# Three passes over the edges of a graph: all row gathers on POOL, and the preparation inside the first pass

## The chip, the cores and the metric

The kernel runs on one core of one Trainium2 chip. The metric is the device time of one execution in microseconds, and the kernel's time is the median of its runs. A profile comes from one execution of its own; its span is the time from the first recorded instruction to the last.

## The reference

Two graph networks follow one another on a graph of N = 12,500 nodes with C = 96 features and 412,500 directed edges (src, dst), sorted by dst. `edge_attr_4` has 4 numbers an edge, `edge_weight1` one.

```python
# first network (its edge input is the one weight an edge), two convolutions with e shared
e = relu(edge_attr @ W_l0 + b_l0) @ W_l1 + b_l1
def gine_conv(x, W1, b1, W2, b2):
    agg = segment_sum(relu(x[src] + e), dst)
    return relu(relu((x + agg) @ W1 + b1) @ W2 + b2)
x = layernorm(x + h2)                 # h2: relu of the second convolution of relu of the first
# second network; mlp(h) = gamma * (h - mean) * rsqrt(var + eps) + beta of relu(h @ W + b), over all rows
message = mlp(concat([x[src], x[dst], mlp(edge_attr_4)]))
x = layernorm(x + segment_sum(message, dst) + mlp(x))
```

So each of three passes over all edges reads one row of 96 numbers by src for every edge, adds a term of the edge, applies a function and sums by dst. The means and variances over all edges are taken in the passes too.

## The kernel before

**Tiling.** The edges stand in tiles of P = 128 (one a partition), T = 26 tiles make a slab, and there are S = 124 slabs. A slab is worked through in 7 chunks, six of CH = 4 tiles and one of 2. V = 4 slabs, that is Q = 28 chunks, are one iteration of a loop written out in full; 31 iterations are one pass. `edge_pass` builds three of them: the first (names conv0_..., table x_rows), the second (conv1_..., table h_rows; `stats=True`, it also takes the statistics of the edge features, from the loads of ea_parts) and the last (last_..., table p_rows). Each has a form for windows, which the data allow and which runs, and a general one that does not run here. `finish` closes the kernel.

**Who does what in a pass.** POOL gathers the rows of a tile with one indirect DMA: `gather`, L268, called from `gpsimd_windows` (L1278 ff.), 26 tiles a slab into one of four buffers `got[j]`, by the node numbers in `idx[j]`. Before the tiles of a chunk it waits until VectorE has added the same chunk of the iteration before (semaphore `add`), and before a slab also for its node numbers (`idx`, L265 loads them). TensorE computes per chunk the hidden layer of the edge term (L540), the product into `ps_pre` (L1314) and the sums by destination; VectorE adds the gathered rows to `ps_pre` (`add_gathered`, L638, once a chunk, signals `add`), cuts the result into parts (L586, L597) and makes the one-hot matrices (L1390); ScalarE applies the relus. Per-chunk matters run one behind another over the engines with semaphores, without an order fixed beyond each engine's own program.

**SyncE's program** (`sync_windows`, L1151 ff.) sets the order around the change. For each slab it runs `next_idx` (loads the node numbers of the slab two further on, after waiting in `landed` for the gathers that read the old ones), then `slab_rows` (after waiting until the hidden layer of the slab two back is done: three loads of w_parts or ea_parts, six in the second pass, L520 and L526), then, from the second slab of the iteration on, `far_rows`. The last tile of the iteration's fourth slab (FAR_J = 3, FAR_T = 25) isn't gathered by POOL: `far_idx_load` brings its 128 node numbers, and `far_rows` reads them into registers, 8 at a time (L1209), and issues one DMA of one row for each (L1213), 42, 43 and 43 at three places. The first place waits until all adds of the iteration before are done. Thus POOL gathers 103 of an iteration's 104 tiles. VectorE waits for the rows (semaphore `far`) before the last add of the fourth slab.

**The preparation** is a block of its own, "setup" (L294 ff.): node numbers and first rows of the nodes are loaded, POOL gathers the first two slabs (52 tiles), VectorE computes window bases, counts what falls outside the windows (`inside`, float32) and the verdict `fits`, writes `near`, and clears the last rows of `sums` (L408). Two small products on TensorE have banks of their own. After the block's end all engines begin the first pass, whose programs start with clearing buffers (L651 to L654) and cutting the weights into bf16 parts (L678).

**The row of counts.** `sums` has a row C for counts. After the second pass's loop POOL clears it (`zero_counts`, L1111, called in `gpsimd_end`) for the last pass.

Of the kernel before, what the change touches and what calls it, by code (L numbers as in the profile page):

```python
# [18 lines left out]
F32 = mybir.dt.float32  # L19
# [6 lines left out]
P = 128  # L26
# [10 lines left out]
FAR_J, FAR_T = V - 1, T - 1  # L37
FAR_PLACES = V - 1
FAR_LOAD = 8
# [113 lines left out]
def gnn_kernel(nc, a, out):  # L153
# [22 lines left out]
    with ctx:  # L176
# [117 lines left out]
        with ExitStack() as st:  # L294
            dst_i = sb("dst_i", [P, S * T], I32, st)
            dst_n = sb("dst_n", [S, T * P], I32, st)
            near_f = sb("near_f", [S, T * P], F32, st)
            near_b = sb("near_b", [S, T * P], BF16, st)
            inside = sb("inside", [P, T * P], F32, st)
            heads = sb("heads", [1, HEADS], I32, st)  # L300
            heads_s = sb("heads_s", [S, NC_], I32, st)
            head_s = sb("head_s", [S, NC_], F32, st)
            head_f = sb("head_f", [1, HEADS], F32, st)
            base_f = sb("base_f", [1, S], F32, st)
            due = sb("due", [1, S], F32, st)
            ahead = sb("ahead", [1, S], F32, st)
            ps = pools(st, base=1, count=1)
            s = Sems(st, "setup")
# [10 lines left out]
            @block.sync  # L319
            def _(sp):  # L320
                for j in range(V):
                    load_slab_idx(sp, early_idx[j], j, early[f"idx{j}"])
                sp.dma_start(heads[:], a["heads"]).then_inc(s["heads"], 16)
                sp.dma_start(heads_s[:], a["heads_s"]).then_inc(s["heads"], 16)
                sp.dma_start(due[:], a["due"]).then_inc(s["heads"], 16)
                sp.dma_start(dst_i[:], a["dst_t"]).then_inc(s["dst"], 16)
                sp.dma_start(dst_n[:], a["dst_n"]).then_inc(s["near"], 16)
                sp.wait_ge(s["near"], 32)
                sp.dma_start(near, near_b[:]).then_inc(early["nearout"], 16)
                sp.wait_ge(early["nearout"], 16)  # L330

            @block.scalar
            def _(act):

                act.dma_start(w_parts[3:4, :], a["is_edge"]).then_inc(s["ones"], 16)
                act.dma_start(ea_parts[3 * D:3 * D + 1, :], a["is_edge"]).then_inc(s["ones"], 16)
                act.wait_ge(s["dst"], 16)
                act.wait_ge(s["near"], 32)
                act.dma_start(sums[0:C, :], a["x_cols"]).then_inc(early["cols"], 16)
                act.wait_ge(s["ones"], 32)  # L340

            @block.tensor
            def _(pe):
                pe.wait_ge(s["base"], 1)
                pe.matmul(ps["base"][0][:, 0:S], ones[0:1, :], base_f[:], start=True, stop=True).then_inc(s["pe"], 1)
                pe.wait_ge(s["cnt"], 1)
                pe.matmul(ps["count"][0][:, 0:4], ones[:], tmp[:, 10:14], start=True, stop=True).then_inc(s["pe"], 1)

            @block.vector
            def _(v):  # L350
                go, done = chain(v, s["dve"])
# [4 lines left out]
                v.wait_ge(s["heads"], 48)  # L356
# [6 lines left out]
                v.drain().then_inc(s["base"], 1)  # L363
                go(v.tensor_copy(base_i[:], base_f[:]))
                go(v.tensor_copy(head_i[:], head_f[:]))
                v.wait_ge(s["dst"], 16)
# [6 lines left out]
                v.wait_ge(s["pe"], 1)  # L373
                go(v.tensor_copy(base_all[:], ps["base"][0][:, 0:S]))
                done()
                rel3 = rel[:].rearrange("p (s t) -> p s t", t=T)
                go(v.tensor_tensor(rel3, rel3, ps["base"][0][:, 0:S].unsqueeze(2).to_broadcast([P, S, T]), ALU.subtract))
# [9 lines left out]
                v.wait_ge(s["near"], 16)  # L387
# [5 lines left out]
                v.tensor_copy(near_b[:], near_f[:]).then_inc(s["near"], 16)  # L393
                count(12, near_f[:], 0.0)
                count(13, near_f[:], float(R))
                v.drain().then_inc(s["cnt"], 1)
                v.wait_ge(s["pe"], 2)
                go(v.tensor_copy(tmp[0:1, 4:8], ps["count"][0][0:1, 0:4]))
# [10 lines left out]
                done()  # L409


        def edge_pass(name, table, y=None, split_edges=False, stats=False, last=False):
# [8 lines left out]
            with ExitStack() as st:  # L421
                idx = early_idx
# [10 lines left out]
                far_idx = sb(f"{name}_far_idx", [1, P], I32, st)  # L433
# [44 lines left out]
                if split_edges:  # L478
                    cols = sb("cols", [C, STEP], F32, st)
                    rows_out = sb("h1_out", [P, NODE_TILES * C], F32, st)  # L480
                    w_f = sb(f"{name}_w_f", [P, COLS], F32, st)
                    w_p = [sb(f"{name}_w_p{i}", [P, COLS], BF16, st) for i in range(3)]
                    e_f = sb(f"{name}_e_f", [P, D * PIECE], F32, st)
                    e_p = sb(f"{name}_e_p", [P, 3 * D * PIECE], BF16, st)
                    hid_f = [sb(f"hid_f{i}", [k, C], F32, st) for i, k in enumerate((KW, KE))]
# [1434 lines left out]
```

## Time and profile before

| | us |
|---|---|
| median of 3 runs | 20690.47 (20690.3 to 20700.37) |
| the profiled execution | 20513.53 |
| its span | 20511.7 |
| TensorE's mean granted clock in it | 0.66 |

The profile gives, for each engine (PE is TensorE, PEld its weight loads, DVE VectorE, ACT ScalarE, POOL GpSimd, SP SyncE), busy time and instructions; a q behind a name (SPq) means the instructions that the engine's sequencer handles, such as the issue of a DMA. Line numbers are those of the kernel before. In a row of the timeline stand the start, the duration, the engine, the line, the operation with output and input, and in brackets how long the engine was idle before it and what ended that. "issue" there is idleness for which the profile shows no cause, "remote" one that ended with another engine's signal. A row of the stretches (windows) counts the instructions of one line that start in a stretch.

### The profile page before, as it was taken

The page shows a single profiled execution, that of the slowest core. Times are in us where ns is not written, and L with a number is a line of the kernel's source. Part 1 is how long each engine was busy: PE and PEld are TensorE (multiplying, and loading weights), DVE is VectorE, ACT ScalarE, POOL GpSimd, SP SyncE. Part 2 cuts the span into 40 slices and gives each one's busy share as a digit, 9 for nine tenths or more (in the row PEclk, how much of TensorE's full clock was granted, in tenths as well). Part 3 has the DMA queues.
Part 4 walks back from the last instruction along what each step waited for, and adds up shares of the span by engine and source line. Part 5 has one row for each costly group of instructions (what it writes and reads, how often), then busy time and mean ns, then how long its engine had stood idle before and what let it go on. Part 6 is the DMA issues. An engine that isn't in the chain of part 4 may idle for free. (4 is left out here: it accounts for less than half of the span.)

```text
span 20511.7 us, 195475 instructions
## 1 busy us (share of the span) xinstructions
PE 9556.3 (47%) x34164; PEld 6799.3 (33%) x34164; DVE 7552.5 (37%) x15603; ACT 4963.2 (24%) x11020; POOL 9073.7 (44%) x9633
## 2 busy tenths in 40 slices
PE   3444444444454554555555555634344434443444
PEld 2333333333333333333333333422233323322333
DVE  3232223232232333333333333434344444443445
ACT  1121212122121222222222222222222222222223
POOL 4444444444444444444444444344444444444443
PEclk9999999999998555555555555555555555555555
DMA  2111111111111111111111111111111111111111
GB/s 61 30 28 31 29 31 29 31 29 31 30 29 40 31 31 30 32 33 33 32 33 32 33 33 32 29 34 29 31 30 30 30 30 30 29 29 31 29 29 33
DMA packets 615379, 650.24 MB, mean 32 GB/s; under 512 B 446921, under 2 KB 447402, under 8 KB 613947
## 3 DMA queue, kind: packets, MB, share of 16 engines
q0 software_dynamic: 306528, 471.44, 10.9%
q1 hardware_dynamic: 256342, 144.36, 2.9%
q10 hardware_dynamic: 51712, 27.54, 0.5%
q14 instruction: 750, 6.14, 0.1%
q8 instruction: 47, 0.77, 0.0%
HBM read 604.73 MB, written 39.43 MB: 31 GB/s over the span
## 5 line engine op out<-in xcount | busy, mean ns | idle before, releaser
L1314 PE MATMUL ps_pre<-w_e,conv_hid 97*128 97x96 f32 x12896 | 3281.4, 434 | 3688.8 <-issue 2145.0
L1314 PEld LDWEIGHTS ps_pre<-w_e,conv_hid 97*128 97x128 f32 x12896 | 2878.0, 327 | 4421.1 <-issue 4029.8
L1314 PE MATMUL ps_pre<-last_w_q,last_hid 128*128 128x96 f32 x6448 | 1628.1, 432 | 2747.0 <-issue 1720.4
L268 POOL DMA_INDIRECT early_got<-p_rows,early_idx x1612 | 1520.7, 943 | 2441.8 <-issue 1449.0
L268 POOL DMA_INDIRECT early_got<-h_rows,early_idx x1612 | 1521.4, 944 | 2190.8 <-issue 1414.2
L1314 PEld LDWEIGHTS ps_pre<-last_w_q,last_hid 128*128 128x128 f32 x6448 | 1440.3, 327 | 3132.6 <-issue 2479.4
L638 DVE TENSOR_TENSOR ps_pre<-ps_pre,early_got 128x384 f32<-128x384 f32 x1302 | 698.0, 536 | 4808.9 <-remote 2284.1
L268 POOL DMA_INDIRECT early_got<-in_x_rows,early_idx x1612 | 1525.0, 946 | 1952.6 <-issue 1243.7
L579 ACT ACTIVATE conv_part<-ps_pre 128x384 bf16<-128x384 f32 x1736 | 815.9, 470 | 5996.6 <-DVE ps_pre L638 3514.7
L268 POOL DMA_INDIRECT conv_got<-h_rows,early_idx x1581 | 1491.5, 943 | 1604.5 <-issue 1383.6
L268 POOL DMA_INDIRECT last_got<-p_rows,early_idx x1581 | 1492.0, 944 | 1530.7 <-issue 1530.4
L268 POOL DMA_INDIRECT conv_got<-in_x_rows,early_idx x1581 | 1491.6, 943 | 1446.8 <-issue 1445.6
L540 PE MATMUL ps_hid<-conv_row,w_hid 12*96 12x512 bf16 x1736 | 1086.2, 626 | 1794.2 <-issue 1346.3
L603 PE MATMUL ps_win<-conv_part,conv_hot 128*112 128x288 bf16 x6448 | 1907.0, 446 | 0.6 <-DVE conv_part L597 0.5
L553 ACT ACTIVATE conv_hid<-ps_hid 96x512 f32<-96x512 f32 x1736 | 974.2, 561 | 3554.5 <-DMA dst_n<-in_dst_n 1126.2
L1390 DVE TENSOR_TENSOR conv_hot<-ps_own,rel 128x448 bf16<-128x448 f32 x1736 | 1018.0, 586 | 1534.1 <-remote 1083.0
L638 DVE TENSOR_TENSOR ps_pre<-ps_pre,conv_got 128x384 f32<-128x384 f32 x868 | 465.6, 536 | 2408.4 <-remote 1597.0
L603 PEld LDWEIGHTS ps_win<-conv_part,conv_hot 128*112 128x112 bf16 x6448 | 1291.2, 214 | 78.2 <-DVE conv_part L597 2.5
L540 PE MATMUL ps_hid<-last_row,w_hid 40*128 40x512 bf16 x868 | 493.7, 569 | 1361.9 <-DVE last_hid L1362 681.4
L540 PEld LDWEIGHTS ps_hid<-conv_row,w_hid 12*96 12x96 bf16 x1736 | 260.1, 150 | 2513.3 <-issue 2095.8
L625 DVE BATCH_NORM_STATS2 conv_parts<-conv_feat 96x6 f32<-96x512 f32 x868 | 564.4, 650 | 1164.6 <-issue 593.8
L603 PE MATMUL ps_win<-last_part,last_hot 128*112 128x291 bf16 x3224 | 964.0, 450 | 0.6 <-DVE last_part L597 0.5
(255 smaller groups left out, 11507.6 us busy)
## 6 DMA issues: line engine op xcount, KB each, us to landing
conv_got<-in_x_rows SPq DMA_DIRECT2D x3968, 0.4 KB
conv_got<-h_rows SPq DMA_DIRECT2D x3968, 0.4 KB
last_got<-p_rows SPq DMA_DIRECT2D x3968, 0.4 KB
conv_row<-ea_parts SPq DMA_DIRECT2D x372, 84.5 KB
last_row<-ea_parts SPq DMA_DIRECT2D x372, 84.5 KB
early_got<-in_x_rows,early_idx POOLq DMA_INDIRECT x1612
early_got<-h_rows,early_idx POOLq DMA_INDIRECT x1612
early_got<-p_rows,early_idx POOLq DMA_INDIRECT x1612
```

The lines of the kernel that those rows point to most:

```text
L268: gp.indirect_dma_start(to[:, t * C:(t + 1) * C], None, table, bass.IndirectOffsetOnAxis(index[:, t:t + 1], 0)).then_inc(sem, 16)
L540: pe.matmul(ps["hid"][0][0:HC, 0:nt * P], w_hid[:], row[r][AT:AT + K, t0 * P:(t0 + nt) * P], start=True, stop=True).then_inc(s["hid"], 1)
L553: act.activation(hid[b][0:C, 0:nt * P], ps["hid"][0][0:C, 0:nt * P], ACT.Relu).then_inc(s["rhid"], 1)
L579: act.activation(part_of(q, 0, nt)[:, :, 0:C], m3, ACT.Relu).then_inc(s["part0"], 1)
L603: return pe.matmul(bank[0:W, 0:3 * M].rearrange("p (i c) -> p i c", i=3), hot_b[:, t * W:(t + 1) * W], parts, start=start, stop=stop)
L625: v.bn_stats(parts[:, c * 6:(c + 1) * 6], feat[b][:, 0:nt * P]).then_inc(s["bn"], 1)
L638: v.tensor_tensor(at, at, got[j][:, t0 * C:(t0 + nt) * C], ALU.add).then_inc(s["add"], 1)
L1314: mm = pe.matmul(ps["pre"][q % 2][:, t * C:(t + 1) * C], hid[q % 2][0:P if last else C1, t * P:(t + 1) * P], w_q[j % U][:, c * C:(c + 1) * ...
L1390: v.tensor_tensor(hot[q % 2][:, 0:nt * W].rearrange("p (t w) -> p t w", w=W), iota[:, 0:W].unsqueeze(1).to_broadcast([P, nt, W]), rel[:, b ...
```

## The change

Three things are changed.

1. POOL gathers all 104 tiles of an iteration. `far_idx_load`, `far_rows`, their buffer and their waits go, on SyncE and on VectorE.
2. The preparation is no block of its own any more. A class `Preparation` holds its buffers, and its parts stand at the head of the first pass's programs. Its buffer `inside` is bf16, its two products go to the bank `ps["e"]`. SyncE loads the preparation's data, then the weights, stores `near`, loads the constants, and waits for `nearout` and for VectorE's new signal `set_fits` before it branches into the windows' form; POOL gathers the first 52 tiles and then waits for `set_fits` too. ScalarE copies the weights before it loads x_cols.
3. VectorE clears the row of counts at the head of the second pass (in `prepare`), where POOL did at its end.

```diff
-FAR_J, FAR_T = V - 1, T - 1
-FAR_PLACES = V - 1
-FAR_LOAD = 8
-def group_tiles(g, j=None):
+def group_tiles(g):
     first, last = GROUPS[g]
-    return CHUNKS[first][0], sum(CHUNKS[last]) - (1 if j == FAR_J and g == len(GROUPS) - 1 else 0)
+    return CHUNKS[first][0], sum(CHUNKS[last])
...
-            block = st.enter_context(nc.Block())
-            @block.gpsimd
-            def _(gp):
+        class Preparation:
+            def gathers(self, gp, s):
...
+            def windows(self, v, s, base_bank, count_bank):
...
                 go(v.tensor_copy(fits[:], tmp[0:1, 2:3]))
                 go(v.memset(sums[C:C + 2, :], 1.0))
                 done()
+                v.drain().then_inc(s["set_fits"], 1)
...
                         go(v.memset(zeros[:], 0.0))
+                        go(v.memset(sums[C:C1, :], 0.0))
...
-                def zero_counts(gp):
-                    gp.memset(sums[C:C1, :], 0.0).then_inc(s["zero_counts"], 1)
-                    gp.wait_ge(s["zero_counts"], 1)
...
                     def body(k, late, final=False):
-                        far_idx_load(k)
...
                             next_idx(k, j, final)
                             slab_rows(k, j)
-                            if j > 0:
-                                far_rows(k, j - 1)
...
-                                if j == FAR_J and g == len(GROUPS) - 1:
-                                    v.wait_ge(s["far"], 16 * P * (k + 1))
...
                 def _(sp):
                     if split_edges:
+                        prep.loads(sp, s)
                         sp.dma_start(w_f[:], a["w_nat"].rearrange("o p i -> (o p) i")).then_inc(s["wf"], 16)
                         for to, src in hid_loads:
                             sp.dma_start(to[:], src).then_inc(s["hf"], 16)
+                        prep.store_near(sp, s)
                         for to, src in consts:
                             sp.dma_start(to[:], src).then_inc(s["const"], 16)
+                        sp.wait_ge(s["nearout"], 16)
+                        sp.wait_ge(s["set_fits"], 1)
...
                 def _(gp):
+                    if split_edges:
+                        prep.gathers(gp, s)
+                        gp.wait_ge(s["set_fits"], 1)
...
                         act.wait_ge(s["wf"], 16)
                         for bank, at in cuts:
                             act.copy(bank, w_f[:, at]).then_inc(s["wx"], 1)
                             act.copy(w_p[0][:, at], w_f[:, at]).then_inc(s["wp0"], 1)
+                        prep.load_cols(act, s)
```

SyncE in the loop of the first pass, before: the loads of the second slab's edge rows (w_parts), the first block of single rows, and the node numbers of the slab two further on (`conv_far_idx` holds the 128 node numbers of the far tile).

```order
L520 ISA [waits conv0_hid]
L520 DMA conv_row<-w_parts 4x3328 x3
L1203 ISA
L1209 TENSOR_LOAD conv_far_idx [waits conv0_faridx,conv0_add]
L1213 ISA
L1213 DMA conv_got<-in_x_rows 1x96
...
L1162 REGISTER_ALU [waits early_got00,early_got01,early_got02,early_got03,early_got04,early_got05]
L265 ISA [waits early_got06]
L265 DMA early_idx<-in_src_t 128x26
```

The same place after:

```order
L521 ISA [waits conv0_hid]
L521 DMA conv_row<-w_parts 4x3328 x3
L1159 ISA
L1159 REGISTER_ALU [waits early_got00,early_got01,early_got02,early_got03,early_got04,early_got05]
L261 ISA [waits early_got06]
L261 DMA early_idx<-in_src_t 128x26
```

The 42 rows, each with the instruction that makes its address, and the register loads are gone; the index load follows the row loads directly.

VectorE at the end of the preparation and the beginning of the first pass, before:

```order
L407 CAST fits<-tmp 1x1 [waits setup_dve]
L408 MEMSET sums 2x12800
L294 UNCONDITIONAL_BRANCH [waits setup_dve]
L1652 UNCONDITIONAL_BRANCH [waits barrier_Pool_Activation_PE_DVE_SP_release]
L651 MEMSET conv_hid 64x512 x2
L653 MEMSET conv_part 128x388
```

The same place after:

```order
L403 CAST fits<-tmp 1x1 [waits conv0_set_dve]
L404 MEMSET sums 2x12800
L652 MEMSET conv_hid 64x512 [waits conv0_set_dve]
L652 MEMSET conv_hid 64x512
L654 MEMSET conv_part 128x388
```

The wait for all other engines between the two is gone.

## Rows read from the trace of the kernel before

**Rows 1.** The page's first part: busy time (share of span) x instructions.

```profile
PE 9556.3 (47%) x34164; PEld 6799.3 (33%) x34164; DVE 7552.5 (37%) x15603; ACT 4963.2 (24%) x11020; POOL 9073.7 (44%) x9633
```

**Rows 2.** Stretches, L638 alone: length, DVE busy (count), PEclk, DMA share, GB/s.

```profile
2000.00:6000.00 4000.00, 287.27 (x534) 1.00 0.14 30
8000.00:12000.00 4000.00, 273.58 (x512) 0.50 0.15 32
15000.00:19000.00 4000.00, 262.00 (x488) 0.50 0.14 30
```

**Rows 3.** The same view, stretches without gathers in the three passes.

```profile
3390.90:3417.90 27.00, 4.33 (x8) 1.00 0.10 19
9814.50:9838.00 23.50, 3.13 (x6) 0.50 0.01 2
9752.60:9773.30 20.70, 2.83 (x5) 0.50 0.04 11
16915.00:16938.80 23.80, 3.19 (x6) 0.50 0.03 6
```

**Rows 4.** The same view, stretches inside long bursts of gathers.

```profile
3005.00:3063.00 58.00, 1.50 (x3) 1.00 0.19 40
8616.00:8643.00 27.00, 0.57 (x1) 0.50 0.19 41
```

**Rows 5.** Timeline of POOL, a gather that follows another.

```profile
9233.40 0.94 POOL L268 DMA_INDIRECT conv_got<-h_rows,early_idx  x1 [0.30 <-issue]
```

**Rows 6.** L1213 in 3010:3062 (gathers) and 3069:3084 (none): ns min/median/max, starts.

```profile
L1213 SPq DMA_DIRECT2D conv_got<-in_x_rows x13: 13/701/1401, 3011.3 to 3059.6; - x13
L1213 SPq DMA_DIRECT2D conv_got<-in_x_rows x25: 3/225/270, 3070.8 to 3083.4; - x25
```

**Rows 7.** Timeline of SyncE and POOL round one block of rows, second pass.

```profile
12126.16 22.09 SPq L1213 DMA_DIRECT2D conv_got<-h_rows  x42
12148.97 0.36 SPq L265 DMA_DIRECT2D early_idx<-in_src_t  x1
12151.32 0.94 POOL L268 DMA_INDIRECT early_got<-h_rows,early_idx  x1 [24.38 <-DMA early_idx<-in_src_t]
```

**Rows 8.** Waits of POOL: us in total, times, longest us.

```profile
POOL early_got L268 <- DMA early_idx<-in_src_t: 2416.7, 89, 34.3
```

**Rows 9.** Timeline of POOL, the first gathers of two short bursts.

```profile
8574.07 0.94 POOL L268 DMA_INDIRECT conv_got<-h_rows,early_idx  x1 [9.38 <-DVE ps_pre L638]
9232.16 0.94 POOL L268 DMA_INDIRECT conv_got<-h_rows,early_idx  x1 [5.41 <-DVE ps_pre L638]
```

**Rows 10.** Timeline of VectorE, the adds round these bursts.

```profile
8572.75 0.55 DVE L638 TENSOR_TENSOR ps_pre<-ps_pre,conv_got 128x384 f32<-128x384 f32 x1
8584.77 0.37 DVE L638 TENSOR_TENSOR ps_pre<-ps_pre,conv_got 128x192 f32<-128x192 f32 x1 [4.25 <-remote]
9230.81 0.57 DVE L638 TENSOR_TENSOR ps_pre<-ps_pre,conv_got 128x384 f32<-128x384 f32 x1 [18.36 <-remote]
9241.04 0.57 DVE L638 TENSOR_TENSOR ps_pre<-ps_pre,conv_got 128x384 f32<-128x384 f32 x1
9246.76 0.34 DVE L638 TENSOR_TENSOR ps_pre<-ps_pre,conv_got 128x192 f32<-128x192 f32 x1
```

**Rows 11.** Timeline of VectorE, from the preparation to the weights.

```profile
59.57 10.72 DVE L408 MEMSET sums<- 2x12800 f32 x1 [2.72 <-issue]
...
85.96 1.02 DVE L651 MEMSET conv_hid<- 64x512 f32 x2 [15.67 <-PEq L201]
...
93.66 0.65 DVE L678 TENSOR_TENSOR ps_hid<-ps_hid,conv_w_p 128x461 f32<-128x461 f32 x1 [3.28 <-issue]
```

**Rows 12.** Timeline of POOL at the end of the second pass.

```profile
13224.74 10.76 POOL L1112 MEMSET sums<- 1x12800 f32 x1
```

**Rows 13.** Timeline of TensorE and VectorE at the head of the second pass.

```profile
6553.76 0.65 PE L540 MATMUL ps_hid<-conv_row,w_hid 12*96 12x512 bf16 x1 [27.22 <-DMA conv_row<-w_parts]
6557.03 0.69 DVE L625 BATCH_NORM_STATS2 conv_parts<-conv_feat 96x6 f32<-96x512 f32 x1 [19.88 <-issue]
```

More of the change, by code:

```diff
@@ L291, in split, with __init__ @@
                     done()
[L294 to L308, printed above, removed]
-            block = st.enter_context(nc.Block())
-            @block.gpsimd
-            def _(gp):
+        class Preparation:
+            def __init__(self, where):
+                self.dst_i = sb("dst_i", [P, S * T], I32, where)
+                self.dst_n = sb("dst_n", [S, T * P], I32, where)
+                self.near_f = sb("near_f", [S, T * P], F32, where)
+                self.inside = sb("inside", [P, T * P], BF16, where)
+                self.heads = sb("heads", [1, HEADS], I32, where)
+                self.heads_s = sb("heads_s", [S, NC_], I32, where)
+                self.head_s = sb("head_s", [S, NC_], F32, where)
+                self.head_f = sb("head_f", [1, HEADS], F32, where)
+                self.base_f = sb("base_f", [1, S], F32, where)
+                self.due = sb("due", [1, S], F32, where)
+                self.ahead = sb("ahead", [1, S], F32, where)
+                self.near_b = sb("near_b", [S, T * P], BF16, where)
+            def gathers(self, gp, s):
                 for j in range(EARLY):
@@ L317, in _, with loads @@
                             gather(gp, a["x_rows"], early_got[j], early_idx[j], t, early[f"got{j}{g}"])
-            @block.sync
-            def _(sp):
+            def loads(self, sp, s):
+                dst_i, dst_n, heads, heads_s, due = self.dst_i, self.dst_n, self.heads, self.heads_s, self.due
                 for j in range(V):
                     load_slab_idx(sp, early_idx[j], j, early[f"idx{j}"])
[L323 to L328, printed above, removed]
-                sp.dma_start(near, near_b[:]).then_inc(early["nearout"], 16)
-                sp.wait_ge(early["nearout"], 16)
@@ L332, in _ @@
[L332 to L338, printed above, removed]
-                act.dma_start(sums[0:C, :], a["x_cols"]).then_inc(early["cols"], 16)
[L340 to L347, printed above, removed]
@@ L386, in _ @@
                 count(11, rel[:], float(W))
-                v.wait_ge(s["near"], 16)
+                v.wait_ge(s["set_near"], 16)
                 for c, (t0, nt) in enumerate(CHUNKS):
@@ L421, in edge_pass @@
             with ExitStack() as st:
+                if split_edges:
+                    w_f = sb(f"{name}_w_f", [P, COLS], F32, st)
+                    w_p = [sb(f"{name}_w_p{i}", [P, COLS], BF16, st) for i in range(3)]
+                    e_f = sb(f"{name}_e_f", [P, D * PIECE], F32, st)
+                    e_p = sb(f"{name}_e_p", [P, 3 * D * PIECE], BF16, st)
+                    hid_f = [sb(f"hid_f{i}", [k, C], F32, st) for i, k in enumerate((KW, KE))]
+                    pick = [sb(f"pick{i}", [k, 3], F32, st) for i, k in enumerate((KW, KE))]
+                    hid_p = [sb(f"hid_p{i}", [KE, C], BF16, st) for i in range(3)]
+                    hid_t = sb("hid_t", [KE, C], F32, st)
+                    tail_f = sb("tail_f", [KE + 1, R], F32, st)
+                    hid_loads = [(hid_f[0], a["w_hid0"]), (hid_f[1], a["w_hid1"]), (pick[0], a["pick0"]),
+                                 (pick[1], a["pick1"]), (tail_f, a["tail"])]
+                    with ExitStack() as place:
+                        prep = Preparation(place)
                 idx = early_idx
@@ L1288, in body @@
                                     continue
-                                for t in range(*group_tiles(g, j)):
+                                for t in range(*group_tiles(g)):
                                     gather(gp, table, got[j], idx[j], t, s[f"got{j}{g}"])
@@ L1653, in _ @@
                 def _(v):
+                    if split_edges:
+                        prep.windows(v, s, base_bank, count_bank)
                     prepare(v)
```

90 lines of the change are left out of this document (43 added, 47 removed).

## The prediction

> **What bounds the kernel now.** I began with the page's engine shares. No engine is near full: TensorE 47%, POOL 44%, VectorE 37%, ScalarE 24% of 20,511.7 us [rows 1]. What costs is therefore a wait that the shares hide, and I looked for it in the loop that fills the run: 31 iterations of 28 chunks in each of three passes, 93 in all. The adds of the gathered rows (L638, one a chunk) count chunks. In 4000 us of the middle of each pass there are 534, 512 and 488 [rows 2], so an iteration takes 4000 x 28 / 534 = 209.7, 218.8 and 229.5 us, mean 219.3.
>
> The same count in stretches where POOL gathers nothing gives the pace of the compute engines by themselves: 27.0/8 = 3.4 us a chunk in the first pass, (23.5 + 20.7)/11 = 4.0 in the second, 23.8/6 = 4.0 in the third [rows 3]; the granted clock there is 1.00 in the first and 0.50 in the others (2.4 and 1.2 GHz). An iteration at that pace would take 94.5, 112.5 and 111.1 us, mean 106. In the middle of a long burst of gathers the count falls to 3 chunks in 58 us and 1 in 27 [rows 4]. A gather starts every 0.94 + 0.30 = 1.25 us [rows 5], so 103 of them take 128.5 us, and (219.3 - 106)/128.5 = 0.88 of POOL's gathering time is added to the iteration: **compute and gathering nearly take turns**. I call that share f. By passes it is 0.90, 0.83 and 0.92.
>
> SyncE shows that this is no matter of data or buffers. Its single-row DMAs for the 104th tile start a median of 701 ns each while POOL gathers and 225 ns when it doesn't, though nothing there waits for a semaphore [rows 6]. Every engine's supply of instructions seems to dry up when POOL gathers; what an engine does in the first microseconds of a burst it does at nearly full pace.
>
> **The change, part by part. SyncE's rows go.** On SyncE a block of 42 or 43 rows stands behind the loads of each of three slabs, and the next slab's index load stands behind the block. In the second pass the block runs from 12,126.16 for 22.1 us, the index load follows at 12,148.97, and the waiting POOL starts 2.3 us later after 24.4 us of idleness [rows 7]; such waits sum to 2416.7 us in 89 cases, and their last releaser is the index load [rows 8]. Without the block that load comes some 23 us earlier. By then 26 tiles (one slab) are free in the buffers today, and POOL gathers them in one burst, or 51 in two slabs together. Earlier loads make POOL wait for the buffers instead: chunk c of a slab may be gathered once VectorE has added chunk c of the slab four back, so POOL gathers **four tiles behind each add**.
>
> What such short bursts cost the trace shows only at a few places of the second pass. (a) Two chunks' tiles at once, 8 x 1.25 = 10 us from 8574.07 [rows 9]: two chunks take 8572.75 to 8584.77 = 12.0 us for 8.0 at pace [rows 10], 4.0 us lost in 10, f = 0.40. (b) Four tiles 5 us after a long burst, 9232.16: the chunk takes 9230.81 to 9241.04 = 10.2, 6.2 lost in 5.0, f = 1.24. (c) The four tiles after that: 9241.04 to 9246.76 = 5.7, 1.7 lost in 5.0, f = 0.34 [rows 9, 10]. So a burst that meets filled engines costs little, and one that meets drained ones more than its own length. At 1.25 x 104 = 129.8 us of gathers to 106 of compute, bursts will follow one another closely. I take a cycle of three chunks: two gathered through at (a)'s price, after which the engines are drained, and one at (b)'s; after it POOL has stood still for about 4 us and they are filled again. f = (4.0 + 6.2)/15.0 = 0.68. The bounds are 0.40 (all as (a)) and 1.24 (all as (b)).
> - Now: 0.88 x 128.5 = 113.3 us an iteration above the compute.
> - Then: 0.68 x 129.8 = 88.3. Difference 25.0, times 93 = **2325 us less**.
>
> The 104th gather is in this (1.25 us a time). The DMA engines move the same 128 rows either way: 0. The 128 row DMAs and 16 register loads that SyncE no longer issues delayed nobody but the index and row loads.
>
> **The preparation moves into the first pass's programs.** VectorE's last piece of it, the clearing of sums, ends at 59.57 + 10.72 = 70.3; the pass's first instruction starts at 85.96 after 15.7 us of waiting for the other engines to leave the block, and the splitting of the weights at 93.66 [rows 11]. Without the block's end VectorE goes straight on, and all behind it moves up by 85.96 - 70.3 = 15.7. I take **16 us less**; bounds 0 (the loads behind it on SyncE and ScalarE, whose order changes, come no earlier) and 19 (the 3.3 us of idleness before 93.66 goes too). SyncE and POOL now wait for VectorE's verdict on the windows before they branch; behind that wait stand the row and piece loads, which wait for the same moment today at the block's end, while the 52 first gathers are ahead of it. 0.
>
> **VectorE clears the row of counts.** The same operation takes 10.8 us on POOL [rows 12], where it goes: 0, since POOL is not what the end of the second pass is late for. On VectorE it stands at the head of that pass, where VectorE is idle for 19.9 us and TensorE waits 27.2 us for the row load [rows 13]: hidden, with some 5 us to spare; 10.8 if SyncE's loads come at once.
>
> **The sum.** 20,511.7 - 2325 - 16 = 18,171 us of span, and 1.8 outside it as in the profiled run (20,513.5). The median of the runs, 20,690.47, is 1.0086 times that run; 18,173 x 1.0086 = **18,330 us**.
>
> **The rivals.**
> - *Full alternation* (0.13). Drained after every short burst: (b) and (c) in turn, f = (6.2 + 1.7)/10 = 0.79, 10.8 us an iteration, 19,660. For it: this is the order in which the trace has the two. Against it: (a) goes through 10 us.
> - *Turns are kept* (0.13). The bursts stay long, or the shape doesn't matter: f stays 0.88. Then only the gather itself counts, 93 x 1.25 x 0.88 = +102 us, with the 16: 20,780. For it: f is the same within 0.1 in three passes of different pace. Against: rows (a) and (c), and the index load that now comes early. The Trainium skill ("DMA: Bandwidth & Descriptors", Issuing engines are not separate DMA queues) says that spreading DMAs over engines saves only their issuing time; by that rule the change would be this rival and no more, and what speaks against it is the order on SyncE, not the transfer.
> - *Slower: the engines are never refilled* (0.12). Place: the 4 or 5 us between two short bursts in any pass. Price: 6.2 us a group, (b). With a share x of such groups f = 0.40 + 0.84x, and the change loses from f = 113.3/129.8 = 0.87, that is x = 0.56. At x = 0.8, f = 1.07: 23,070; at x = 1: 25,140. For it: POOL's long idle spells, in which all engines run free today, are gone. Against: in (c) 5 us of rest were enough.
> - *Full overlap, or nearly* (0.07). All groups as (a): 14,920. If the engines didn't disturb each other at all, POOL's 129.8 us and the 3 us around them would be the iteration, 20,511.7 - 93 x 86.3 - 16, 12,580 by the median's scale. The stretches inside bursts [rows 4, 6] speak against it. The Trainium skill ("Runtime: NRT & Kernel Launch", Instruction fetch mechanics) says that each sequencer fetches its next page by DMA while it executes and that this is mostly hidden; by that rule this would be the result, with a chance of its own of 0.02, since the trace disagrees (701 ns against 225).
>
> **How the numbers follow.** The forecast's own case, f between 0.56 (one group in five drained) and 0.76, is 16,900 to 19,300 and has 0.55. Alternation takes 19,300 to 20,640 with 0.13, the kept turns lie round 20,780 with 0.13, together 0.81: the range is 16,900 to 20,850. Left out are the fast end (0.07) and the slow one (0.12). About 0.2% is what a measurement of this kernel can tell from no change. Faster by more: 0.55 + 0.13 + 0.07 = 0.75. Same, out of the kept turns where their gather is partly covered: 0.03. Slower: 0.10 + 0.12 = 0.22.
>
> **What would show it.** Right: no DMA of rows on SyncE, POOL's idleness moved from the index load to the adds of L638, gathers mostly in fours with a gap between, and more adds in the same three stretches of 4000 us (28 x 4000/194.3 = 576 on average instead of 511). The preparation is right if the weight splits start at about 78 us, the counts if the first statistics of the second pass are no later behind its head. Wrong: bursts of 26 or 52 as before (kept turns), or fours with 10 us to a chunk (never refilled). The whole rests on the cost of short bursts, which five or six places of one pass at the slow clock show.

## The result: 16,125 us, below the range

The changed kernel takes 16,125.5 us (median of 4 runs, 16,119 to 16,157) beside 20,690.4 for the kernel before: ratio 0.779, 95% interval 0.778 to 0.780. The forecast was 18,330 with a range from 16,900: the direction and the place were right, the size was too small by 2200 us.

The first part of the changed kernel's page gives each engine's busy time:

```profile
PE 9557.2 (59%) x34164; PEld 6796.8 (42%) x34164; DVE 7534.2 (47%) x15604; ACT 4921.9 (30%) x11020; POOL 9148.3 (57%) x9725
```

The same busy times as in [rows 1] now lie in a shorter span (16,155.1). The adds of the gathered rows (L639 now) in 4000 us of each pass, with the columns of [rows 2]:

```profile
1000.00:5000.00 4000.00, 379.73 (x706) 1.00 0.19 38
6000.00:10000.00 4000.00, 346.75 (x652) 0.50 0.19 41
11000.00:15000.00 4000.00, 333.10 (x622) 0.50 0.18 38
```

An iteration takes 4000 x 28/706 = 158.6, 171.8 and 180.1 us, mean 170.2, where it took 219.3: 49 us less, times 93 = 4560 us. The medians differ by 4565 us and the spans of the two traces by 20,511.7 - 16,155.1 = 4357, so the iterations are the difference, as nearly as stretches from the middle of each pass can tell. The share f of POOL's 129.8 us that is added to the compute (94.5, 112.5 and 111.1 us) is 0.49, 0.46 and 0.53, mean 0.49, against 0.68 in the forecast and 0.88 before.

POOL's waits (us in total, times, longest):

```profile
POOL early_got L264 <- DVE ps_pre L639: 1637.9, 392, 19.2
POOL conv_got L264 <- DVE ps_pre L639: 1076.4, 296, 6.0
...
POOL last_got L264 <- DVE ps_pre L639: 558.7, 100, 11.8
...
POOL early_got L264 <- DMA early_idx<-in_src_t: 201.3, 32, 10.9
POOL last_got L264 <- DMA early_idx<-in_src_t: 195.6, 32, 7.9
...
POOL conv_got L264 <- DMA early_idx<-in_src_t: 38.7, 9, 5.8
```

The wait for the index load went from 2416.7 us [rows 8] to 201.3 + 195.6 + 38.7 = 436, and the wait for VectorE's adds, 3273 us in the three rows, took its place, as forecast. Not as forecast is the shape of the bursts. The next rows are from one cycle in the first pass: first POOL's gathers that follow a gap, then VectorE's adds and its instructions after an idle time.

```profile
3044.53 0.94 POOL L264 DMA_INDIRECT early_got<-in_x_rows,early_idx  x1 [3.75 <-DVE ps_pre L639]
...
3062.72 0.94 POOL L264 DMA_INDIRECT early_got<-in_x_rows,early_idx  x1 [3.52 <-DVE ps_pre L639]
...
3065.97 0.94 POOL L264 DMA_INDIRECT early_got<-in_x_rows,early_idx  x1 [1.06 <-issue]
```

```profile
3043.19 0.57 DVE L639 TENSOR_TENSOR ps_pre<-ps_pre,early_got 128x384 f32<-128x384 f32 x1 [9.07 <-remote]
...
3046.39 0.57 DVE L639 TENSOR_TENSOR ps_pre<-ps_pre,early_got 128x384 f32<-128x384 f32 x1 [1.17 <-PE ps_pre L1287]
...
3050.53 0.57 DVE L639 TENSOR_TENSOR ps_pre<-ps_pre,early_got 128x384 f32<-128x384 f32 x1 [1.97 <-PE ps_pre L1287]
...
3056.06 0.62 DVE L1363 TENSOR_TENSOR conv_hot<-ps_own,rel 128x448 bf16<-128x448 f32 x1 [4.50 <-remote]
...
3061.58 0.37 DVE L639 TENSOR_TENSOR ps_pre<-ps_pre,early_got 128x192 f32<-128x192 f32 x1 [4.43 <-remote]
```

The burst that starts at 3044.53 has 12 gathers (12 x 1.25 = 15 us): two adds come inside it at nearly the pace, POOL goes on to the tiles that they free at once, and then VectorE makes no further add until the burst's last gather, which starts at 3058.26, is over. Three chunks took 3043.19 to 3061.58 = 18.4 us. The next burst starts 3.5 us after the last and has two gathers, the one after it comes after another 1.1 us and has 12 again, and the first two chunks beside it are at pace once more. In this way the 26 tiles of a slab come as 12, 2 and 12, in the first pass and for the most part in the second; in the third there are bursts of 20, 16, 6 and 4.

### The profile page after: what moved, and what is told of

The parts are those of the page before. It is cut to its first block and busy times, and to the rows that moved or that the text cites. A ratio compares the mean times of both kernels' runs of the same rounds, so it can differ in the third digit from the quotient of the medians.

```text
span 16155.1 us, 157576 instructions
## 1 busy us (share of the span) xinstructions
PE 9557.2 (59%) x34164; PEld 6796.8 (42%) x34164; DVE 7534.2 (47%) x15604; ACT 4921.9 (30%) x11020; POOL 9148.3 (57%) x9725
## 5 line engine op out<-in xcount | busy, mean ns | idle before, releaser
L639 DVE TENSOR_TENSOR ps_pre<-ps_pre,early_got 128x384 f32<-128x384 f32 x1302 | 697.6, 536 | 2385.5 <-remote 803.5
L639 DVE TENSOR_TENSOR ps_pre<-ps_pre,conv_got 128x384 f32<-128x384 f32 x868 | 464.3, 535 | 1427.7 <-remote 823.5
L598 DVE TENSOR_TENSOR conv_part<-ps_pre,conv_part 128x384 bf16<-128x384 f32 x1736 | 904.5, 521 | 65.8 <-issue 60.5
```

What stands on the lines that cost most here:

```text
L598: v.tensor_tensor(part_of(q, 2, nt)[:, :, 0:C], tiles_of(ps["pre"][b], nt, C), part_of(q, 1, nt)[:, :, 0:C], ALU.subtract).then_inc(s["par ...
L639: v.tensor_tensor(at, at, got[j][:, t0 * C:(t0 + nt) * C], ALU.add).then_inc(s["add"], 1)
```

## The experiments

**Two levels.** The same kernels turned out to run at two levels, by the chip: on four chips the kernel before takes 20,501 to 20,670 us, on two others 12,108 and 12,131. The measurement above and the trace before are of the first kind (the high level). Each result below says which it was, and each ratio is against the kernel before on the same chip.

### The rows alone (e1, e11)

```diff
 # the kernel before, with
-                        far_idx_load(k)
-                            if j > 0:
-                                far_rows(k, j - 1)
```

> The kernel before with the rows alone taken from SyncE: POOL gathers all 104 tiles, the preparation stays a block of its own and POOL clears the counts. If the rows are the whole gain, 16,125 plus the 6 us by which the changed kernel's first add comes earlier: 16,130, within 0.2%. If the moved preparation or the clearing matters beyond the head, more than 16,160 or less than 16,100.

Measured at the low level: 12,244.6 beside 12,130.9, ratio 1.009 (1.008 to 1.011), 114 us more.

> The kernel of e1 again (only the rows taken from SyncE; the preparation and the clearing of the counts as before). At the high level it should take the whole gain but for the 6 us by which the first add of the changed kernel comes earlier: 16,130, ratio 0.780. If the moved preparation or the clearing carries a part of the gain, 16,200 or more. At the low level 1.009 as in e1.

Measured at the high level: 16,116 beside 20,670, ratio 0.780 (0.778 to 0.781). The rows carry the whole gain (the changed kernel has 0.779); the other two parts of the change are worth nothing that can be measured here.

### The changed kernel at the low level (e5)

> The changed kernel itself, beside the kernel before. In the first series the kernel before took 12,131 us, not 20,690, and POOL's gathers set its iteration (128.5 us a time). Theory 'two levels': where the gathers don't hold up the other engines, the iteration is POOL's own time, and the change adds the 104th gather, 93 x 1.25 = 116 us, less some 6 to 10 us at the head: 12,131 goes to 12,240, ratio 1.009; where they do, 20,690 goes to 16,125, ratio 0.78. Rival: the change gains here too, if less: under 12,100.

Measured: 12,210.3 beside 12,108.4, ratio 1.008 (1.007 to 1.010): on this chip the change makes the kernel **slower**, by 0.8%. The adds (L639) in 3000 us of each pass:

```profile
1000.00:4000.00 3000.00, 348.08 (x647) 1.00 0.23 48
5000.00:8000.00 3000.00, 345.96 (x647) 0.50 0.25 55
9000.00:12000.00 3000.00, 346.91 (x647) 0.50 0.24 52
```

3000 x 28/647 = 129.8 us in all three passes, at either clock: 104 gathers of 1.248 us. POOL gathers without a stop and is the bound, and the 104th gather costs its 1.25 us 93 times: 116 us, of which 102 show here and 114 in e1.

### Long bursts without rows (e2, e7, e12)

In e2 and e7 POOL waits per slab, in e12 for two slabs, one and one:

```diff
 # e2, e7: the changed kernel, with
-                                if not opening(k):
-                                    gp.wait_ge(s["add"], Q * (k - 1) + NC_ * j + end + 1)
+                                if not opening(k) and g == 0:
+                                    gp.wait_ge(s["add"], Q * (k - 1) + NC_ * (j + 1))
 # e12
+                                if not opening(k) and g == 0 and j != 1:
+                                    gp.wait_ge(s["add"], Q * (k - 1) + NC_ * (j + (2 if j == 0 else 1)))
```

> The changed kernel, but POOL waits before a slab until all seven chunks of the slab four back are added, so that it gathers 26 tiles in a row again; SyncE has no rows. Theory 'length': the other engines go on for the first 8 us or so of a burst and stand for its rest. 26 tiles last 32.4 us and cost about 24 each, 4 x 24 + 106 = 202 us an iteration, 19,000 us in all. Rival 'rows': what slowed the kernel before were SyncE's rows by themselves (their instructions and DMAs), whatever the bursts look like: 16,100 to 16,600, and L638's count in the first pass stays near 700 in 4000 us.

Measured at the low level: 12,228.7 beside 12,130.9. POOL is the bound there, and the length of the bursts makes no difference.

> The kernel of e2 again (the changed kernel with bursts of 26 tiles). The runs so far show two levels: the kernel before at 20,690 us, where gathers hold up the other engines, and at 12,110 to 12,130, where they don't. If this run's kernel before is at the high level: theory 'length' 19,000 us, theory 'rows' 16,100 to 16,600. If it is at the low one: 12,230 as before, and neither is told apart.

Measured at the high level: 19,196 beside 20,668 (one run).

> The changed kernel, but POOL waits so that it gathers 52, 26 and 26 tiles in a row, nearly the bursts of the kernel before (51, 26, 26), with no rows on SyncE. At the high level: if the length of the bursts is the whole cause, 20,700; if SyncE's rows themselves took a part, less, and not below e7's 19,196: I expect 19,700 to 20,100, that is 600 to 1000 us for the rows themselves. At the low level 12,230 to 12,400.

Measured at the high level: 19,936 beside 20,670, ratio 0.965 (0.963 to 0.966). The adds in 4000 us of each pass, e7 and then e12:

```profile
1000.00:5000.00 4000.00, 312.01 (x580) 1.00 0.16 32
7000.00:11000.00 4000.00, 289.48 (x545) 0.50 0.16 34
14000.00:18000.00 4000.00, 279.47 (x521) 0.50 0.15 32
```

```profile
1000.00:5000.00 4000.00, 294.23 (x547) 1.00 0.14 31
7000.00:11000.00 4000.00, 279.95 (x526) 0.50 0.15 33
14000.00:18000.00 4000.00, 274.06 (x511) 0.50 0.14 31
```

With the old bursts and no rows (e12) an iteration is 204.8, 212.9 and 219.2 us. Of the 4554 us between the kernel before and e11 on the same chip (20,670 and 16,116), 19,936 - 16,116 = 3820 come with the length of the bursts, and 20,670 - 19,936 = 730 with SyncE's rows themselves. Bursts of 26 alone (e7) cost 3080 us against e11. The 730 are a net figure, since e12 has the 104th gather and the kernel before has not. Theory "length" holds; the rival "rows" has the smaller part.

### What holds the engines up (e4, e6, e8, e14)

Ahead of the changed kernel stand four blocks in which ScalarE and VectorE run small instructions while POOL gathers, or doesn't: empty ones in e4, copies of 128x1 in e6 and e8. POOL waits until its gathers have landed after every 26. The cut shows the copies of e6 and e8:

```diff
+                            if loop:
+                                with eng.Fori(0, 60) as k:
+                                    for i in range(8):
+                                        op(bass.ds(k * 8 + i, 1))
+                            else:
+                                for i in range(480):
+                                    op(slice(i, i + 1))
```

> The changed kernel with four short blocks ahead of it: ScalarE runs 1000 empty instructions in a straight line and VectorE the same number as a loop of ten, without gathers and beside 104 gathers, and then the other way round. If POOL's gathers hold up the fetching of instructions, the straight line takes several times longer beside gathers (about 700 ns an instruction, as SyncE's rows did) and the loop does not. If they hold up every instruction that a sequencer handles (or its semaphores), both do. If the first instructions of a straight line only are quick, a long line goes at full pace for some microseconds and then stands.

e4 ran at the low level and told nothing of this: the empty instructions of its straight line didn't stay in the program.

> The changed kernel with four short blocks ahead of it: ScalarE runs 480 small copies in a straight line and VectorE 480 small copies in a loop of eight, first without gathers, then beside 104 of them, and then with the forms exchanged. Where the kernel before takes 12,100 us: neither form is slower beside gathers, by more than a tenth. Where it takes 20,700: if the fetching of instructions is what gathers hold up, the straight lines take several times longer beside them (towards 700 ns an instruction, as SyncE's rows did) and the loops don't; if every instruction is held up, both do.

Low level: 480 copies in a straight line on ScalarE took 44.7 us with and without gathers, and VectorE's loop made 474 copies in 76 us both times.

> The kernel of e6 again (blocks of 480 small copies in a straight line and in a loop, without and beside gathers). In e6, at the low level, neither form was slower beside gathers: 93 and 161 ns an instruction with and without them. At the high level: if what is held up is the fetching of code, the straight line takes towards 700 ns an instruction and the loop stays at its pace; if all engines share one limited rate of instructions while POOL gathers, straight line and loop are both slow, after a first 100 or so at full pace.

High level. VectorE's copies in stretches: its loop without gathers, beside them, in the 11 us after their end and then; its straight line without gathers and beside them.

```profile
4.00:80.00 76.00, 61.13 (x473) 1.00 0.00 0
100.00:216.00 116.00, 10.47 (x68) 1.00 0.19 38
217.00:228.00 11.00, 1.08 (x7) 1.00 0.04 9
230.00:270.00 40.00, 32.12 (x248) 1.00 0.00 1
289.00:317.00 28.00, 28.00 (x466) 1.00 0.00 1
370.00:484.00 114.00, 12.58 (x82) 1.00 0.19 38
```

From 6.2 copies a microsecond the loop falls to 0.6, and from 16.6 the straight line to 0.7. The loop goes through the same eight instructions again and again and is held up as much as the straight line, so it is not the fetching of new code that is slow. Both forms come at a small rate: with ScalarE's 0.7, some 1.3 copies a microsecond for both engines, where straight lines on both make 27. Only in the first 5 us or so are they at pace, some 90 copies of the two engines together here. Whether the two engines share one rate or each has its own, no run tells, since none had one of them alone. And behind the 104 gathers, whose three pauses of 1.8 us don't show in the rate, the copies stay slow for 11 us after the last one. The Trainium skill ("Runtime: NRT & Kernel Launch", Instruction fetch mechanics) says that fetching is mostly hidden: the straight line of 480 copies at 16.6 a microsecond without gathers agrees, and the hold-up is another one. If the prediction's "supply of instructions" meant the fetching of code, it named the wrong thing.

e14 asks what in a gather does it:

```diff
+                phase("probe1", "memsets")   # 12 memsets of 2496 numbers on POOL, no DMA
+                phase("probe2", "rows")      # 78 gathers of 128 rows
+                phase("probe3", "plain")     # SyncE: plain DMAs in pieces of 384 bytes
+                phase("probe4", "half")      # 78 gathers of 64 rows
```

> The changed kernel with four blocks ahead of it, each with 480 small copies on ScalarE and on VectorE: beside POOL memsets and no DMA; beside 78 gathers of 128 rows; beside plain DMAs that SyncE issues and that move pieces of 384 bytes as the gathers do, with POOL idle; beside 78 gathers of 64 rows. At the high level: if it is POOL's being busy that holds up the others, the memsets do it too; if it is the DMA packets (102 a microsecond in the gathers), the plain DMAs do it as well and the half gathers less; if it is the gathers' being prepared on POOL, only the second and fourth block are slow, and equally. At the low level all four are at full pace.

High level. VectorE's copies beside each of the four:

```profile
4.00:32.00 28.00, 28.00 (x465) 1.00 0.01 2
60.00:120.00 60.00, 7.28 (x53) 1.00 0.18 38
194.00:222.00 28.00, 28.00 (x465) 1.00 0.62 184
290.00:370.00 80.00, 9.28 (x61) 1.00 0.11 20
```

POOL's being busy does nothing (16.6 copies a microsecond). Plain DMAs from SyncE at 184 GB/s and 62% of the DMA engines do nothing. Gathers at 38 GB/s bring it to 0.9, and those of half as many rows to 0.8: it comes with the gather as POOL issues it, not with the number of its rows or its bytes. A plain DMA issued by POOL was not tried. What in the gather does it, and why some chips don't show it, stays open. So does one rival: every execution timed here was also recorded by the profiler, and whether that recording has a part in the hold-up was not tested.

### More instructions on SyncE (e9)

```diff
                             slab_rows(k, j)
+                            with sp.Fori(0, 20) as i:
+                                sp.nop(nofuse=True)
```

> The changed kernel with a loop of 20 passes, that is 40 register and branch instructions, on SyncE behind the loads of each slab: 160 more instructions an iteration and no data moved. Theory 'shared rate': at the high level all engines together get some 2 to 4 instructions a microsecond in the later part of a burst, so 160 more take 40 to 60 us of it: 170 goes to 200 us or more an iteration, 18,500 to 20,500. Rival 'length of bursts alone': under 17,000. At the low level: no change, 12,210.

Measured at the high level: 16,900 beside 20,668 (one run), some 8 us an iteration more than the changed kernel. That is under the rival's 17,000 and far from 18,500, so the price that the theory gave for 160 instructions was far too high. The 8 us can't even be put down to the instructions themselves, because they also make the index load late: POOL's waits for it are 757.0 + 538.4 + 399.3 = 1695 us, where the changed kernel has 436, and in the first pass there are bursts of 16 and 20 gathers again. No run tells the two causes apart.

### Two tiles on SyncE (e10)

The kernel before with the last two tiles of the fourth slab, 256 rows, on SyncE:

```diff
-    return CHUNKS[first][0], sum(CHUNKS[last]) - (1 if j == FAR_J and g == len(GROUPS) - 1 else 0)
+    return CHUNKS[first][0], sum(CHUNKS[last]) - (2 if j == FAR_J and g == len(GROUPS) - 1 else 0)
```

> The other way round: the kernel before, with the last two tiles of every four slabs, not one, loaded row by row by SyncE, so that POOL gathers 102. At the low level POOL's gathers are the iteration, and it falls by 1.25 us: 12,120 less 116 is 12,005, ratio 0.990, if SyncE's 256 rows (225 to 270 ns each, some 65 us) fit beside it. At the high level more rows on SyncE make the kernel slower: over 23,000.

Measured at the high level: 27,487 beside 20,668, ratio 1.330 (1.328 to 1.332). It had no run at the low level. SyncE's timeline, first pass:

```profile
3236.63 99.37 SPq L1216 DMA_DIRECT2D conv_got<-in_x_rows  x84
3336.65 0.36 SPq L265 DMA_DIRECT2D early_idx<-in_src_t  x1
...
3340.41 80.64 SPq L1216 DMA_DIRECT2D conv_got<-in_x_rows  x86
...
3425.40 80.14 SPq L1216 DMA_DIRECT2D conv_got<-in_x_rows  x86
```

SyncE issues rows for 99 + 81 + 80 = 260 of an iteration's 286 us, and the index load stands behind a whole block. In the kernel before, the same three blocks of the first pass take 77, 53 and 54 us; the 22 us of [rows 7] are a block that lay in a gap between two bursts. The first of the three:

```profile
3007.05 76.61 SPq L1213 DMA_DIRECT2D conv_got<-in_x_rows  x42
```

This is the chain of the prediction, turned up: the index load is late, so POOL is late, so all tiles of a slab come in one burst (50, 26 and 26 gathers here), and the rows are slowed by that burst.

### How long a rest it takes (e3, e13, e16, e17, e18)

```diff
                                 for t in range(*group_tiles(g)):
                                     gather(gp, table, got[j], idx[j], t, s[f"got{j}{g}"])
+# e3, e17: always;  e16: if g in (1, 3, 5)
+                                t0, t1 = group_tiles(g)
+                                gp.wait_ge(s[f"got{j}{g}"], 16 * (t1 - t0) * (k + 1))
+# e13
+                                with gp.Fori(0, 4):
+                                    gp.nop(nofuse=True)
+# e18: if g in (1, 3, 5)
+                                    gp.memset(spare[:], 0.0).then_inc(s["spare"], 1)   # 128x768
```

> The changed kernel, but after each chunk's gathers POOL waits until they have landed (about 2 us), so that no burst is longer than four tiles. Theory 'length': the stalls inside bursts go; the adds then come evenly, and the time is set by POOL, 28 chunks of 5.0 us and 2 us of pause: 180 to 190 us an iteration, 16,900 to 17,900, while a chunk's own time beside a burst stays at pace plus 1 us. Rival 'sum': each gather costs the others the same share wherever it stands (0.5 of its time), and a pause only adds room: 16,100 to 16,300.

Low level: 17,823 beside 12,131, 190 us an iteration. POOL is the bound there and the pauses only cost; it says nothing on the theories.

> The changed kernel with a loop of four passes on POOL behind each chunk's gathers (about 1 us), so that no burst is longer than four tiles. At the high level: if 1 us is enough to clear what the gathers hold up, the iteration is POOL's own, 129.8 + 28 x 1.1 = 161 us, and the kernel 15,200; if it isn't, the stalls stay and the pauses come on top, 16,500 to 18,000. At the low level 161 us an iteration, 15,100.

High level: 16,310 beside 20,670, ratio 0.789 (0.788 to 0.791). Inconclusive: the loop made no gap. In the first pass the gathers start 1.25 us apart in bursts of 12 and 2 as in the changed kernel.

> The changed kernel, but after the second, fourth and sixth chunk of each slab POOL waits until their gathers have landed (2.2 us, as the pauses of e3 cost), so that no burst is longer than 8 to 10 tiles. At the high level: if such a pause after 10 us of gathers lets the other engines go on at pace, the iteration is POOL's time with its pauses, 129.8 + 12 x 2.2 = 156 us, and the kernel 14,800, which would beat both; if a pause of 2.2 us clears little, the stalls stay and the kernel takes 16,100 to 17,500. At the low level 156 us an iteration, 14,700, slower than both.

High level: **14,593** beside 20,660, ratio 0.706 (0.705 to 0.708), which beats both kernels there. POOL's gathers behind a gap, and VectorE's adds beside the first of them:

```profile
3001.41 0.94 POOL L264 DMA_INDIRECT early_got<-in_x_rows,early_idx  x1 [2.43 <-issue]
...
3013.48 0.94 POOL L264 DMA_INDIRECT early_got<-in_x_rows,early_idx  x1 [2.39 <-DVE ps_pre L639]
```

```profile
3007.70 0.57 DVE L639 TENSOR_TENSOR ps_pre<-ps_pre,early_got 128x384 f32<-128x384 f32 x1 [4.13 <-DMA early_got<-in_x_rows,early_idx]
...
3012.70 0.57 DVE L639 TENSOR_TENSOR ps_pre<-ps_pre,early_got 128x384 f32<-128x384 f32 x1 [2.32 <-DMA early_got<-in_x_rows,early_idx]
```

Eight gathers take 12.07 us with their pause, 2.1 more than without. VectorE waits mostly for rows: its idle time before the adds that ended with "remote" is 503 us in all, where the changed kernel has 1627. All three passes count 628 to 631 adds in 3500 us, 155 to 156 us an iteration at either clock, which is POOL's time with its pauses (129.8 + 12 x 2.1 = 155). The hold-up no longer sets the time.

> The kernel of e3 again (a pause of 2.2 us after each chunk's gathers). At the low level it took 190.3 us an iteration, POOL's time with 28 pauses. At the high level the same 190 us and 17,820, if pauses after 5 us keep the other engines wholly free; 195 us or more, over 18,200, if they don't.

High level: 17,805 beside 20,660, ratio 0.862 (0.860 to 0.863): 190.3 us an iteration, the same as e3 at the low level. With a rest after every 5 us of gathers the levels don't differ.

> The kernel of e16 with a shorter pause: after the second, fourth and sixth chunk of each slab POOL clears 768 numbers a partition of a spare tile and waits for that, some 0.7 us (2.18 us for 2496 in the probe of e14) and its hand-over, in place of 2.2 us. At the high level: if 1 us after 10 us of gathers is enough, the iteration is 129.8 + 12 x 1.0 = 142 us and the kernel 13,400; if the other engines need more, their stalls come back and it takes 14,600 to 16,500. At the low level 142 us, 13,400.

High level: 15,262 beside 20,501, ratio 0.745 (0.744 to 0.746). Its pauses are 1.35 us (gathers 2.60 apart), and the adds in 3500 us of each pass are

```profile
1000.00:4500.00 3500.00, 342.44 (x637) 1.00 0.19 40
6000.00:9500.00 3500.00, 333.28 (x624) 0.50 0.21 46
11500.00:15000.00 3500.00, 307.18 (x573) 0.50 0.18 40
```

that is 153.8, 157.0 and 171.0 us where POOL with its pauses would be 129.8 + 12 x 1.35 = 146. After bursts of 8 to 10 gathers a rest of 1.35 us is a little too short, one of 2.1 is enough.

## Why the prediction was wrong

- **What bounds the kernel.** Right at the high level, and this is what the experiments confirm best: in the kernel before, compute and gathering nearly take turns, and the turns are made by the length of bursts (e7, e12). The changed kernel's iteration is 129.8 us without the hold-up (e5) and 170 with it.
- **The index load behind the rows.** Right: removing the rows alone gives the whole gain (e11), and most of POOL's wait moved from the index load to the adds.
- **The price of short bursts.** The step that failed. The prediction took bursts like (b) [rows 9, 10] for one group in three, at 6.2 us lost in 5.0, and so had f = 0.68. In the cycle of the first pass no such group follows a short burst: a burst of 12 gathers takes 18.4 us for three chunks of 3.4, 8.2 us lost in 15, and the two gathers between cost next to nothing; f is 0.49 over all. The 0.19 between the two are 0.19 x 129.8 x 93 = 2290 us, as much as the whole miss. Why (b) misled is argued, not tested: it came 5 us behind a burst of 42 gathers, and in e8 the engines stay slow for 11 us behind 104, while behind a short burst 2.1 us of rest are enough (e16). The trace of the kernel before has the aftermath without any gather beside it. A burst of 26 ended at 9143.62, the next began at 9174.62, and the chunk between these two adds took 7.3 us instead of 4.0:

```profile
9145.97 0.57 DVE L638 TENSOR_TENSOR ps_pre<-ps_pre,conv_got 128x384 f32<-128x384 f32 x1 [18.35 <-remote]
...
9153.25 0.57 DVE L638 TENSOR_TENSOR ps_pre<-ps_pre,conv_got 128x384 f32<-128x384 f32 x1 [0.71 <-PE ps_pre L1314]
```

  But behind most other bursts of 26 the first chunk was near its pace. Row (a) came behind a burst of 42 as well, but after 9.4 us of rest where (b) had 5.4 [rows 9], so the two fit together if what a burst of 42 needs lies between them. Rows (a) and (c), 0.40 and 0.34, lie nearer to the 0.49. The prediction named the bound of 0.40 but cut its range at 0.56; two rows against one should have opened it further down.
- **Four tiles behind each add.** Only half right: the second and third add fall into the burst that the first one starts, so the bursts join to 12.
- **The rows' own cost** was put at nothing; it is 730 us net, of 4554 (e12). It is no part of the miss, since the forecast's f for the changed kernel came from other rows.
- **From the trace to the runs.** The prediction multiplied by 1.0086, the runs' median over the traced run, which is 157 us of its 18,330. For the changed kernel the traced run is 0.2% above the median. The kernel before takes 20,501 us on one chip and 20,660 on another, so the factor may well have been one between chips.
- **The preparation.** The first instruction of the pass came forward by 85.96 - 68.37 = 17.6 us, and the splits from 93.66 to 72.70, by 21:

```profile
68.37 1.02 DVE L652 MEMSET conv_hid<- 64x512 f32 x2 [0.27 <-DVE sums L404]
...
72.70 0.62 DVE L680 TENSOR_TENSOR ps_hid<-ps_hid,conv_w_p 128x461 f32<-128x461 f32 x1
```

  But the first add came forward by only 6.3, from 127.93 to 121.58. SyncE stood in the constants' loads beside the gathers, one of them for 27 us, and the row loads behind them came at 110, where they came at 115 before:

```profile
51.92 27.16 SPq L1574 DMA_DIRECT2D w_msg_e<-in_w_msg_e  x1
...
110.01 9.10 SPq L521 DMA_DIRECT2D conv_row<-w_parts  x6
```

  That is between the lower bound that the prediction named, 0, and its value of 16.
- **The row of counts.** Right, hidden: on VectorE 10.72 us, with 7.1 us idle behind it, and the second pass's first add is 47.0 us behind the first pass's last one (46.8 before).

```profile
5064.95 10.72 DVE L662 MEMSET sums<- 1x12800 f32 x1 [2.72 <-issue]
...
5083.31 0.69 DVE L626 BATCH_NORM_STATS2 conv_parts<-conv_feat 96x6 f32<-96x512 f32 x1 [7.11 <-issue]
```

- **The rivals.** "Full overlap", which rows 4 and 6 spoke against with full right at this level, is what the other two chips do: 12,210 against the 12,580 worked out for it. There the 104th gather alone decides, and the kernel gets slower by 102 to 114 us.

## What to carry to other kernels

Where a stall is tied to another engine's activity, find how it depends on the length of that activity and on what came just before, and don't price a case by a row that stands in another's aftermath. A load of indices behind a long block of other DMAs on the same queue turns an even flow of gathers into bursts. Before a tuned balance is built on a hold-up, look whether all chips have it: the same change is worth 0.78 on some and 1.008 on others, and the version with pauses, best on the first kind at 14,593, would have an iteration of some 155 us on the second kind too, which has 130 without them (an estimate from POOL's time, which e3 and e17 show to be the same on both).

## What the runs showed of the hardware

The kernel before takes 20,501 to 20,670 us on four chips and 12,108 and 12,131 on two. On the two chips of the first kind that ran probes (e8, e14), while POOL issues gathers 1.25 us apart, ScalarE and VectorE together get some 1.3 to 1.8 small copies a microsecond after the first 5 us or so (27 without gathers), in loops and in straight lines alike. Gathers of 64 rows do the same as those of 128; POOL memsets and SyncE's plain DMAs at 184 GB/s do nothing. On the chip of the second kind that ran the probe (e6), gathers do nothing either. A rest of 2.1 us after 10 us of gathers keeps the engines at pace and one of 1.35 us not wholly (e16, e18); after 104 gathers with three short pauses it takes 11 us (e8). A gather of 64 rows costs POOL 1.20 us and one of 128 rows 1.25 (e14).
